# Turning the normalised rows of x by one DMA per tile instead of on TensorE, from tile 6 on

## The chip, the cores and the metric

The kernel runs on one core of a Trainium2 chip. The metric is the device time of one execution in microseconds (us). Engines are named as the profile names them: PE is TensorE's matmul side and PEld its weight load, DVE is VectorE, ACT is ScalarE, POOL is GpSimd, SP is SyncE, which here only issues DMAs.

## The reference

2048 tokens of width 512 pass through two gated blocks. The first picks one of four experts by token id, the second is a feed-forward block with fp8 weights.

```python
# xattn: ctx is Wg, Wu and Wd of each of 4 experts, (4, 512, 512)
n = layernorm(x)
for e in range(4):
    g = silu(n @ ctx[e].T); u = n @ ctx[e].T
    y = (g * u) @ ctx[e].T
    out = where(expert_of(token) == e, y, out)
x = x + tanh(g_xattn) * out
# ffn: weights rounded to fp8, per-column scales
n2 = layernorm(x)
x = x + tanh(g_ffn) * ((silu(n2 @ Wgate * gs) * (n2 @ Wup * us)) @ Wdown * ds)
```

## The kernel before, in words

All work is written out by hand, one in-order program for each engine, tied by counting semaphores. The tokens are first sorted by expert, so that each of 16 tiles of 128 tokens (`xs[:, tile]`, fp32, gathered by POOL) holds one expert or a border between two. The first block is then 19 **steps** (16 tiles and 3 borders). Both precisions are made by splitting: a value is a high fp16 part and a low fp16 part (the value less its high part), and a product is three fp16 products.

In step s PE does, in this order: `product_z(s)` (12 matmuls of 128x512, L1333); then, while s < 15, the four 128x128 fp32 transposes of the normalised tile s+1 from `xn` into the PSUM bank `XT` (`transpose4`, L1262, named `bank<-ident,xn`); the four transposes of `h` of step s-1 into `HT` (same line, `bank<-ident,h`); column norms of a weight slab (L1391); and `product_y(s-2)` (12 matmuls, L1314). `product_y(s-2)` waits for `x1_done`, which DVE raises with `add_expert(s-3)` (L1028) at the end of its own step s-1, because both use the one PSUM bank `Y`.

ACT's step s: `silu` (L738) when z(s) is there, `x_high(s+1)` (L681, the high part out of `XT` into `X2[:, s+1, 0]`), `normalise(s+2)` (L676, `xn`), `h_high(s-1)` (L744), then work on the fp8 slabs (L700, L708) and from step 7 the second layernorm (L691, L692). DVE's step s: `product_h` (L1099), `x1_low(s+1)` (L999, reads `XT` in PSUM and `X2`), `h_low(s-1)` (L995), `round_stats` (L978 and the small rows after it: one `bn_stats` of a tile ahead, for s+4 < 16, and from step 6 one for the second layernorm, so steps 6 to 11 have both), `slab_big` (L975) for each of that step's slabs (two in steps 5, 8, 11, 14, 16), and `add_expert(s-2)` (L1028).

POOL works off rounding of the slabs in the same steps: `round_slab` (L581 makes `w_sum` and raises `sum_done`, L584), `ln_scalars(s+4)` (L510, L513, waits for DVE's statistics), and from step 8 `x2_low` (L597).

SP issues every plain DMA and every DMA transpose in one order. After four slab loads come the 12 transposes of the experts' matrices (L438), each expert followed by a wait until they have landed; then for each step `turn_x2(s-8)` (L446, from step 8) and the loads of the step's slabs (`load_slab`, L428), of which load n waits for `sum_done` of slab n-4, whose buffer it fills. The first of these loads, slabs 4 and 5, belong to steps 2 and 3.

The second block (L1415 and L1423) follows: four groups of four tiles, one chain of matmuls. The first operand of `product_y(18)` and of these groups depends on DVE's `ffn_scales` and on `add_expert(17)`, which stand behind the end of POOL's slab work.

Of the kernel before, what the change touches and what calls it, by code (L numbers as in the profile page):

```python
# [16 lines left out]
F32, F16, BF16, I32 = mybir.dt.float32, mybir.dt.float16, mybir.dt.bfloat16, mybir.dt.int32  # L17
ALU = mybir.AluOpType
ACT = mybir.ActivationFunctionType
# [14 lines left out]
def build(nc, x, token_ids, ctx, g_xattn, g_ffn, gate_w, up_w, down_w, gate_scale, up_scale, down_scale, out):  # L34
    B, S, D = x.shape
    TOK = B * S
    TILES = TOK // P
# [9 lines left out]
    EARLY_NORMS = 18  # L47
    LATE_ORDER = ("g2", "d3", "g3", "d4", "g4", "g5", "d5", "g6", "g7", "d6", "d7", "d8", "d9", "d10", "d11")
    TURNS = {25: 11, 27: 12, 29: 13, 31: 14, 33: 15}
    STATS1_LEAD = 4  # L50
    STATS2_LAG = 6
    NORM2_LAG = 7
# [14 lines left out]
    with ExitStack() as stack:  # L67
# [3 lines left out]
        def sem(name):  # L71
            return stack.enter_context(nc.semaphore(name))


        xs = sb("xs", [P, TILES, D], F32)
        M = sb("M", [P, E, 2, KC, 512], F16)
        X2 = sb("X2", [P, TILES, 2, KC, P], F16)
# [182 lines left out]
        y_done = sem("y_done")  # L260
        x1_done = sem("x1_done")
        x2n_done = sem("x2n_done")
        x2T_in = [sem("x2T_in0"), sem("x2T_in1")]
        x2lo_done = sem("x2lo_done")
        abs_done = sem("abs_done")
# [48 lines left out]

        def x2_row(tile, part):
            return x2rows[:, tile % 2, part * D:(part + 1) * D]

        def x2_landed(engine, tile):

# [86 lines left out]
        def _(sp):  # L406
# [24 lines left out]
            def turn_expert(e):  # L431
# [8 lines left out]
                sp.wait_ge(m_in, 16 * KC * e)  # L440
                sp.nop().then_inc(m_ready, 1)

            def turn_x2(tile):

                sp.wait_ge(x2lo_done, tile + 1)
                sp.dma_start_transpose(X2[:, tile].rearrange("p a k i -> p (a k) i"),  # L446
                                       x2rows[:, tile % 2, :]).then_inc(x2T_in[tile % 2], 16)
# [4 lines left out]
            for e in range(1, E):  # L452
                turn_expert(e)
            for s in range(STEPS):
                if s >= X2_LAG:
                    turn_x2(s - X2_LAG)
                for n in slabs_of(s, s):
                    load_slab(loaded)
                    loaded += 1
# [185 lines left out]
        def _(act):  # L645
            a = nc.scalar
# [25 lines left out]
            def normalise(tile):  # L672
                act.wait_ge(ln_done, tile + 1)
                if tile:
                    act.wait_ge(xT_done, tile)
                a.activation(xn[:], xs[:, tile, :], ACT.Identity, scale=ln_tab[:, tile, 0, 0:1],  # L676
                             bias=ln_tab[:, tile, 0, 1:2]).then_inc(xn_done, 1)

            def x_high(tile):
                act.wait_ge(xT_done, tile + 1)  # L680
                a.activation(x2_part(tile, 0), XT[:].rearrange("p (k i) -> p k i", k=KC),  # L681
                             ACT.Copy).then_inc(xhi_done, 1)
# [57 lines left out]
            def h_high(s, lo):  # L740
                act.wait_ge(hT_done, s + 1)
                if lo >= 2:
                    act.wait_ge(y_done, s - 1)
                a.activation(hTh[:, lo % 2, :], HT[:], ACT.Copy).then_inc(hhi_done, 1)  # L744

            def step(s, lo):
                if lo < 2:
                    x_high(s + 1)
                silu(s, lo)
                if 2 <= lo < TILES - 1:  # L750
                    x_high(s + 1)
                if lo + 2 < TILES:
                    normalise(s + 2)
                if lo >= 1:
                    h_high(s - 1, lo - 1)
                if lo + 1 < E:
                    expert_rows_high(lo + 1)
                if lo == 0:
                    squares(3)
                for n in slabs_of(s, lo):  # L760
                    slab_abs(n, slab_slot(n), slab_turn(n), slab_before(n))
                for n in squared_of(s, lo):
                    slab_square(n, n % 2, n)
                if lo >= NORM2_LAG:
                    normalise2(s - NORM2_LAG)
# [74 lines left out]
        def _(dve):  # L840
# [152 lines left out]
            def h_low(s, lo):  # L993
                dve.wait_ge(hhi_done, s + 1)
                v.tensor_tensor(hTl[:, lo % 2, :], HT[:], hTh[:, lo % 2, :], ALU.subtract).then_inc(hlo_done, 1)  # L995

            def x1_low(tile):
                dve.wait_ge(xhi_done, tile + 1)
                v.tensor_tensor(x2_part(tile, 1), XT[:].rearrange("p (k i) -> p k i", k=KC), x2_part(tile, 0),  # L999
                                ALU.subtract).then_inc(xlo_done, 1)  # L1000
# [110 lines left out]
            def step(s, lo):  # L1111
# [2 lines left out]
                product_h(s, lo)  # L1114
                if lo == STEPS - 1:
                    ffn_norms(SMALL, 0, 2)
                if 2 <= lo < TILES - 1:
                    x1_low(s + 1)
                if lo >= 1:
                    h_low(s - 1, lo - 1)  # L1120
                if lo == STEPS - 1:
                    add_expert(s - 2)
                if lo == 0:
# [132 lines left out]
        def _(pe):  # L1256
# [69 lines left out]
                        for k in range(KC) for lhs, rhs in ((0, 0), (0, 1), (1, 0))]  # L1326

            def product_z(s, lo, operands):
                pe.wait_ge(xlo_done, min(s + 1, TILES))
                if lo >= 2:  # L1330
                    pe.wait_ge(h_done, s - 1)
                for n, (lhs, rhs) in enumerate(operands):
                    ins = t_.matmul(Z[lo % 2][:], lhs, rhs, start=(n == 0), stop=(n == 3 * KC - 1))  # L1333
                ins.then_inc(z_done, 1)
# [15 lines left out]
            def step(s, lo):  # L1350

                product_z(s, lo, z_next[0])
                if lo < TILES - 1:
                    pe.wait_ge(xn_done, s + 2)
                    transpose4(XT, xn, xT_done)
                if lo == 0:
# [151 lines left out]
```

## Time and profile before

| | us |
|---|---|
| median of 3 runs | 406.75 (406.28 to 407.37) |
| the profiled execution | 406.11 |
| its span | 404.4 |
| PE busy | 379.4 (94%) |
| DVE busy | 219.1 (54%) |
| ACT busy | 187.3 (46%) |
| POOL busy | 161.2 (40%) |

The profiled execution is 0.64 us under the median; 1.7 us of it lie outside the span. The shares are means over two unlike halves: until about 140 us the 19 steps run on all engines, after that PE works almost alone. The granted clock was 0.995 of full speed over the span.

### The profile page before, as it was taken

How to read it: one execution, taken by the hardware profiler on the slowest of the kernel's cores; microseconds unless marked ns; L12 is line 12 of the kernel's file. 1: busy time of each engine (PE TensorE's matmuls, PEld its weight loads, DVE VectorE, ACT ScalarE, POOL GpSimd, SP SyncE). 2: the span in 40 equal slices, each digit the busy share in tenths (PEclk: the TensorE clock that was granted, in tenths of full speed). 3: DMA queues.
4: the chain of work that ended last, by engine and by line, in shares of the span. 5: the costliest groups of instructions: out<-in, count | busy, mean ns of one | idle time of the engine just before them, and what ended most of it. 6: DMA issues, size and time to landing. Idle time of an engine off the chain costs nothing.

```text
span 404.4 us, 6038 instructions
## 1 busy us (share of the span) xinstructions
PE 379.4 (94%) x1912; PEld 183.2 (45%) x1912; DVE 219.1 (54%) x465; ACT 187.3 (46%) x294; POOL 161.2 (40%) x199
## 2 busy tenths in 40 slices
PE   2889799999999899999999999999999999999990
PEld 2445355545555444444444444444444444444440
DVE  5876888797867786787524222224222225222243
ACT  4777756787886536694432222222222222222220
POOL 2678989997989930411008100006200005300003
PEclk9999999999999999999999999999999999999997
DMA  7697783444445340670002000001100001100002
GB/s 259 167 343 196 138 193 113 68 117 80 105 105 117 94 104 2 151 165 25 0 2 78 28 0 0 2 0 53 52 0 0 0 0 40 66 0 2 0 0 104
DMA packets 40075, 29.99 MB, mean 74 GB/s; under 512 B 31192, under 2 KB 31216, under 8 KB 40048
## 3 DMA queue, kind: packets, MB, share of 16 engines
q1 hardware_dynamic: 37488, 21.26, 22.2%
q0 software_dynamic: 2560, 8.39, 6.1%
q8 instruction: 14, 0.23, 0.3%
q14 instruction: 13, 0.11, 0.1%
HBM read 18.11 MB, written 4.19 MB: 55 GB/s over the span
## 4 chain that ended last, share of the span: by engine, by line
PE 81%; DVE 8%; POOL 3%; issue 3%; ACT 2%; DMA 1%; DVEq 0%; POOLq 0%; ACTq 0%
PE bank L1415 41%; PE bank L1423 20%; PE bank L1314 9%; PE bank L1333 8%; PE bank L1262 2%; POOL xs L502 1%; DVE stats L978 1%; DMA xs<-in_x,order 1%; DVE row_hot L913 1%; ACT xn L676 1%; DVE xs L1243 1%; DVE hTl L995 1%; DVE X L1240 1%; DVE xs L1028 1%; ACT hTh L744 1%
## 5 line engine op out<-in xcount | busy, mean ns | idle before, releaser
L1415 PE MATMUL bank<-X,W 128*128 128x512 f16 (+1 forms) x768 | 173.3, 379 | 0.0
L1415 PEld LDWEIGHTS bank<-X,W 128*128 128x128 bf16 x768 | 75.0, 98 | 90.9 <-ACT late_norms L802 0.5
L1189 DVE SCALAR_TENSOR_TENSOR cs<-bank,up_mul,cs 128x512 f32<-128x512 f32 x48 | 36.0, 751 | 108.7 <-PE bank L1415 104.6
L1423 PE MATMUL bank<-W,cs 128*128 128x512 bf16 x376 | 88.7, 379 | 0.0
L776 ACT ACTIVATE cs<-bank,gate_mul 128x512 f32<-128x512 f32 x48 | 32.9, 686 | 80.0 <-PE bank L1415 80.0
L783 ACT ACTIVATE cs<-cs 128x512 f16<-128x512 f32 x47 | 29.5, 628 | 77.8 <-DVE cs L1189 77.6
L633 POOL TENSOR_TENSOR xs<-xs,X 128x512 f32<-128x512 f32 x12 | 15.3, 1274 | 125.2 <-DVE X L1240 124.9
L1423 PEld LDWEIGHTS bank<-W,cs 128*128 128x128 f16 x376 | 36.5, 98 | 43.7 <-DVE cs L1197 0.2
L1333 PE MATMUL bank<-M,X 128*128 (+1 forms) x228 | 52.3, 379 | 3.1 <-DVE X L999 2.1
L1197 DVE TENSOR_TENSOR cs<-cs 128x512 f16<-128x512 f32 x47 | 33.8, 719 | 31.5 <-ACT cs L783 31.5
L1314 PE MATMUL bank<-M,hTh 128*128 (+1 forms) x152 | 45.1, 378 | 3.2 <-DVE xs L1028 3.2
L639 POOL DMA_INDIRECT out<-xs,order x16 | 16.7, 1045 | 50.9 <-DVE xs L1243 47.5
L1333 PEld LDWEIGHTS bank<-M,X 128*128 (+1 forms) x228 | 22.2, 98 | 30.7 <-issue 5.3
L1314 PE MATMUL bank<-M,hTl 128*128 (+1 forms) x76 | 28.8, 379 | 0.0
L584 POOL TENSOR_TENSOR W<-w_sum,w_big 128x512 bf16<-128x512 f32 x21 | 27.0, 1286 | 1.6
L581 POOL TENSOR_TENSOR w_sum<-ws,w_big 128x512 f32<-128x512 f32 x21 | 26.7, 1271 | 0.7 <-POOL W L584 0.2
L510 POOL TENSOR_TENSOR ln_tab<-prep,ln_half 128x1 f32<-128x1 f32 (+1 forms) x26 | 16.6, 639 | 23.2 <-DVE prep L883 23.0
L738 ACT ACTIVATE silu_z<-bank,z_step 128x512 f32<-128x512 f32 x18 | 12.3, 685 | 23.9 <-PE bank L1333 23.9
L597 POOL TENSOR_TENSOR x2rows<-x2n,x2rows 128x512 f16<-128x512 f32 x16 | 19.3, 1208 | 7.2 <-ACT x2n L692 7.2
L700 ACT ACTIVATE w_big<-ws 128x512 f32<-128x512 f32 x36 | 21.4, 627 | 0.6 <-DMA ws<-in_L_ffn_up_w 0.6
L1314 PEld LDWEIGHTS bank<-M,hTh 128*128 128x128 f16 x152 | 13.6, 97 | 17.7 <-issue 3.9
L1099 DVE SCALAR_TENSOR_TENSOR h<-bank,h_step,silu_z 128x512 f32<-128x512 f32 x18 | 13.5, 750 | 14.8 <-PE bank L1262 8.7
(164 smaller groups left out, 379.8 us busy)
## 6 DMA issues: line engine op xcount, KB each, us to landing
ws<-in_L_ffn_gate_w SPq DMA_DIRECT2D x12, 256.0 KB, 2.7
ws<-in_L_ffn_up_w SPq DMA_DIRECT2D x12, 256.0 KB, 2.7
ws<-in_L_ffn_down_w SPq DMA_DIRECT2D x12, 256.0 KB, 2.9
cs<-in_ctx SPq DMA_DIRECT2D x2, 1024.0 KB, 6.6
X<-in_ctx SPq DMA_DIRECT2D x2, 1024.0 KB, 6.9
xs<-in_x,order POOLq DMA_INDIRECT x16, 4.3
dsc<-in_L_ffn_down_scale SPq DMA_DIRECT2D x1, 256.0 KB, 7.0
X<-x2rows SPq DMA_TRANSPOSE x16, 3.1
```

Source lines behind the costliest of these rows:

```text
L581: g.tensor_tensor(w_sum[:], ws[:, slot], w_big[:, slot], ALU.add).then_inc(sum_done, 1)
L584: g.tensor_tensor(dst, w_sum[:], w_big[:, slot], ALU.subtract).then_inc(q_done, 1)
L597: g.tensor_tensor(x2_row(tile, 1), x2n[:, tile % 2, :], x2_row(tile, 0), ALU.subtract).then_inc(x2lo_done, 1)
L700: a.activation(w_big[:, slot], ws[:, slot], ACT.Abs, scale=FP8_STEP).then_inc(abs_done, 1)
L776: a.activation(sg[:, c % 2, :], GATE[c % 2][:], ACT.Silu, scale=gate_mul[:, c:c + 1]).then_inc(sg_done, 1)
L783: a.activation(fuse_part(g, c, 0), fuse[:, c % 2, :], ACT.Copy).then_inc(fh_done, 1)
L1189: v.scalar_tensor_tensor(out=fuse[:, c % 2, :], in0=UP[c % 2][:], scalar=up_mul[:, c:c + 1], in1=sg[:, c % 2, :], op0=ALU.mult, op1=ALU.mu ...
L1197: v.tensor_tensor(fuse_part(g, c, 1), fuse[:, c % 2, :], fuse_part(g, c, 0), ALU.subtract).then_inc(fl_done, 1)
L1314: ins = t_.matmul(dst[:], lhs, expert_block(e, part, k), start=(n == 0), stop=(n == 3 * KC - 1))
L1333: ins = t_.matmul(Z[lo % 2][:], lhs, rhs, start=(n == 0), stop=(n == 3 * KC - 1))
L1415: ins = t_.matmul(dst[c % 2][:].rearrange("p (t i) -> p t i", t=TPG), w, x2_group(g, part, k), start=(k == 0 and part == 0), stop=(k == KC ...
L1423: ins = t_.matmul(ACC[t][:], fuse_part(g, c, part)[:, t * P:(t + 1) * P], W8[:, down_slab(c), :], start=(c == 0 and part == 0), stop=(c == ...
```

## The change

For tiles 6 to 15 PE no longer transposes. ACT writes the normalised row tile twice in token order (`split_rows`: once as fp16 into `x_row(tile, 0)`, once as fp32 into `xn`), DVE takes the fp16 part off (`x_row_low`, into `x_row(tile, 1)`), and one DMA transpose issued by SP (`turn_x`) writes both parts of the tile into `X2`. The buffers are the front of `cs`, whose first use is over by then. `x_high` and `x1_low` of those tiles fall away. `product_z` of those tiles waits for the DMA (`x_landed`) in place of `xlo_done`.

```diff
+    X_BY_DMA = 6
...
+        def x_row(tile, part):
+            return cs[:, 0, tile % 2].bitcast(F16)[:, part * D:(part + 1) * D]
...
+            def turn_x(tile):
+                sp.wait_ge(xrow_low_done, tile - X_BY_DMA + 1)
+                sp.dma_start_transpose(X2[:, tile].rearrange("p a k i -> p (a k) i"),
+                                       cs[:, 0, tile % 2].bitcast(F16)).then_inc(xT_in[tile % 2], 16)
...
             for s in range(STEPS):
+                if X_BY_DMA <= s + 2 < TILES:
+                    turn_x(s + 2)
                 if s >= X2_LAG:
                     turn_x2(s - X2_LAG)
...
+            def split_rows(tile):
+                act.wait_ge(ln_done, tile + 1)
+                if tile >= X_BY_DMA + 2:
+                    act.wait_ge(xT_in[tile % 2], 16 * ((tile - X_BY_DMA) // 2))
+                mul, add = ln_tab[:, tile, 0, 0:1], ln_tab[:, tile, 0, 1:2]
+                a.activation(x_row(tile, 0), xs[:, tile, :], ACT.Identity, scale=mul, bias=add)
+                if tile == X_BY_DMA:
+                    act.wait_ge(xT_done, tile)
+                else:
+                    act.wait_ge(xrow_low_done, tile - X_BY_DMA)
+                a.activation(xn[:], xs[:, tile, :], ACT.Identity, scale=mul, bias=add).then_inc(xn_done, 1)
...
-                if 2 <= lo < TILES - 1:
+                if 2 <= lo < X_BY_DMA - 1:
                     x_high(s + 1)
-                if lo + 2 < TILES:
+                if lo + 2 < X_BY_DMA:
                     normalise(s + 2)
                 if lo >= 1:
                     h_high(s - 1, lo - 1)
+                if X_BY_DMA <= lo + 2 < TILES:
+                    split_rows(s + 2)
...
+            def x_row_low(tile):
+                dve.wait_ge(xn_done, tile + 1)
+                v.tensor_tensor(x_row(tile, 1), xn[:], x_row(tile, 0), ALU.subtract).then_inc(xrow_low_done, 1)
...
-                if 2 <= lo < TILES - 1:
+                if 2 <= lo < X_BY_DMA - 1:
                     x1_low(s + 1)
                 if lo >= 1:
                     h_low(s - 1, lo - 1)
+                if X_BY_DMA <= lo + 2 < TILES:
+                    x_row_low(s + 2)
...
-                pe.wait_ge(xlo_done, min(s + 1, TILES))
+                pe.wait_ge(xlo_done, min(s + 1, X_BY_DMA))
+                if X_BY_DMA <= lo < TILES:
+                    x_landed(pe, s)
...
-                if lo < TILES - 1:
+                if lo < X_BY_DMA - 1:
                     pe.wait_ge(xn_done, s + 2)
                     transpose4(XT, xn, xT_done)
```

Three places show where instructions now stand. First SP, from the slab loads ahead of the experts' transposes (`M<-W`) on. Before:

```order
10 L428 DMA ws<-in_L_ffn_gate_w 128x512 x4
11 L438 DMA_TRANSPOSE M<-W 128x8x128 x12
12 L428 DMA ws<-in_L_ffn_up_w 128x512 x4
13 L428 DMA ws<-in_L_ffn_gate_w 128x512 x3
14 L446 DMA_TRANSPOSE X<-x2rows 128x8x128
15 L428 DMA ws<-in_L_ffn_gate_w 128x512
16 L428 DMA ws<-in_L_ffn_up_w 128x512
```

And with the change, the same stretch of SP (`X<-cs` is `turn_x`, tile 6 first):

```order
11 L450 DMA_TRANSPOSE M<-W 128x8x128 x12
12 L440 DMA ws<-in_L_ffn_up_w 128x512 x2
13 L458 DMA_TRANSPOSE X<-cs 128x8x128
14 L440 DMA ws<-in_L_ffn_up_w 128x512
15 L458 DMA_TRANSPOSE X<-cs 128x8x128
16 L440 DMA ws<-in_L_ffn_up_w 128x512
17 L440 DMA ws<-in_L_ffn_gate_w 128x512
18 L458 DMA_TRANSPOSE X<-cs 128x8x128
19 L440 DMA ws<-in_L_ffn_gate_w 128x512
```

Each tile's transpose stands between the slab loads: that of tile 6 behind the loads of slabs 4 and 5, that of tile 7 also behind that of slab 6, that of tile 8 also behind those of slabs 7 and 8.

Second DVE, one of its steps 6 to 11 (`hTl` is `h_low`, `X<-bank,X` is `x1_low`, `cs<-xn,cs` is `x_row_low`). Before:

```order
146 L1099 SCALAR_TENSOR_TENSOR h<-bank,h_step,silu_z 128x512
147 L999 TENSOR_TENSOR X<-bank,X 128x512
148 L995 TENSOR_TENSOR hTl<-bank,hTh 128x512
149 L978 BN_STATS stats<-xs 128x6 x2
150 L987 BN_AGGR mv<-stats 128x2 x2
```

With the change:

```order
147 L1138 SCALAR_TENSOR_TENSOR h<-bank,h_step,silu_z 128x512
148 L1030 TENSOR_TENSOR hTl<-bank,hTh 128x512
149 L1034 TENSOR_TENSOR cs<-xn,cs 128x512
150 L1013 BN_STATS stats<-xs 128x6 x2
151 L1022 BN_AGGR mv<-stats 128x2 x2
```

The count is the same. The subtraction that read PSUM is gone, and one that reads two SBUF tensors stands behind `h_low`, ahead of the statistics and of `add_expert`.

Third ACT, the front of the same step. Before:

```order
46 L738 ACTIVATE silu_z<-bank,z_step 128x512
47 L681 ACTIVATE X<-bank 128x512
48 L676 ACTIVATE xn<-xs,ln_tab 128x512
49 L744 ACTIVATE hTh<-bank 128x512
50 L700 ACTIVATE w_big<-ws 128x512
```

With the change:

```order
47 L771 ACTIVATE silu_z<-bank,z_step 128x512
48 L777 ACTIVATE hTh<-bank 128x512
49 L705 ACTIVATE cs<-xs,ln_tab 128x512
50 L710 ACTIVATE xn<-xs,ln_tab 128x512
51 L733 ACTIVATE w_big<-ws 128x512
```

`h_high` moves up to the second place; `xn` is finished by the fourth instruction of the step instead of the third.

## Rows read from the trace of the kernel before

**Rows 1.** The page's chain that ended last, shares by engine.

```profile
PE 81%; DVE 8%; POOL 3%; issue 3%; ACT 2%; DMA 1%; DVEq 0%; POOLq 0%; ACTq 0%
```

**Rows 2.** Timeline of PE, steps 6 to 8: start, length, line, names, count, idle before.

```profile
58.32 2.75 PE L1333 MATMUL bank<-M,X 128*128 x12
60.91 0.60 PE L1262 MATMUL bank<-ident,xn 128*128 128x128 f32 x4
61.35 0.60 PE L1262 MATMUL bank<-ident,h 128*128 128x128 f32 x4
...
67.07 0.60 PE L1262 MATMUL bank<-ident,xn 128*128 128x128 f32 x4
...
68.34 0.59 PE L1314 MATMUL bank<-M,hTh 128*128 x2 [0.15 <-DVE xs L1028]
...
70.92 2.75 PE L1333 MATMUL bank<-M,X 128*128 x12
```

**Rows 3.** Timeline of PE, the transposes of steps 13 and 15.

```profile
105.00 0.60 PE L1262 MATMUL bank<-ident,xn 128*128 128x128 f32 x4
...
117.40 0.60 PE L1262 MATMUL bank<-ident,h 128*128 128x128 f32 x4
```

**Rows 4.** Timeline of SP's DMA issues, 39 to 60 us.

```profile
54.94 2.03 SPq L428 DMA_DIRECT2D ws<-in_L_ffn_up_w  x2
```

**Rows 5.** Timeline of POOL, the sums of slabs 1 and 2.

```profile
55.34 1.27 POOL L581 TENSOR_TENSOR w_sum<-ws,w_big 128x512 f32<-128x512 f32 x1
...
61.26 1.27 POOL L581 TENSOR_TENSOR w_sum<-ws,w_big 128x512 f32<-128x512 f32 x1
```

**Rows 6.** The DMA transposes of `x2rows` (L446, 16 of them), issue to landing.

```profile
DMA to landing us min/median/max: 3.0/3.1/4.7
```

**Rows 7.** Timeline of DVE, step 7 (one slab, both statistics).

```profile
68.24 0.75 DVE L1099 SCALAR_TENSOR_TENSOR h<-bank,h_step,silu_z 128x512 f32<-128x512 f32 x1
...
69.66 0.69 DVE L995 TENSOR_TENSOR hTl<-bank,hTh 128x512 f16<-128x512 f32 x1
70.27 1.28 DVE L978 BATCH_NORM_STATS2 stats<-xs 128x6 f32<-128x512 f32 x2
...
72.19 0.41 DVE L975 TENSOR_SCALAR w_big<-w_big 128x512 f32<-128x512 f32 x1
72.73 0.75 DVE L1028 SCALAR_TENSOR_TENSOR xs<-bank,y_step,xs 128x512 f32 x1
```

**Rows 8.** Timeline of DVE, start of step 15, which has no transposes of x.

```profile
118.33 0.75 DVE L1099 SCALAR_TENSOR_TENSOR h<-bank,h_step,silu_z 128x512 f32<-128x512 f32 x1 [1.49 <-ACT silu_z L738]
```

**Rows 9.** Timeline of ACT, front of step 8.

```profile
73.71 0.69 ACT L738 ACTIVATE silu_z<-bank,z_step 128x512 f32<-128x512 f32 x1 [1.12 <-PE bank L1333]
74.30 0.59 ACT L681 ACTIVATE X<-bank 128x512 f16<-128x512 f32 x1
74.78 0.81 ACT L676 ACTIVATE xn<-xs,ln_tab 128x512 f32<-128x512 f32 x1
75.48 0.59 ACT L744 ACTIVATE hTh<-bank 128x512 f16<-128x512 f32 x1
```

**Rows 10.** Groups by line over the span: busy us, mean ns, idle before.

```profile
L1197 DVE TENSOR_TENSOR cs<-cs 128x512 f16<-128x512 f32 x47 | 33.8, 719 | 31.5 <-ACT cs L783 31.5
...
L975 DVE TENSOR_SCALAR w_big<-w_big 128x512 f32<-128x512 f32 x21 | 14.9, 728 | 0.5 <-ACT w_big L700 0.5
```

**Rows 11.** Timeline of DVE at 165 us.

```profile
165.05 1.64 DVE L1197 TENSOR_TENSOR cs<-cs 128x512 f16<-128x512 f32 x1
```

**Rows 12.** Timeline of POOL at 163 us.

```profile
163.42 2.72 POOL L597 TENSOR_TENSOR x2rows<-x2n,x2rows 128x512 f16<-128x512 f32 x2
169.33 1.16 POOL L597 TENSOR_TENSOR x2rows<-x2n,x2rows 128x512 f16<-128x512 f32 x1 [3.19 <-ACT x2n L692]
```

**Rows 13.** Timeline of DVE, `add_expert(17)`.

```profile
144.61 0.74 DVE L1028 SCALAR_TENSOR_TENSOR xs<-bank,y_step,xs 128x512 f32 x1
```

**Rows 14.** Timeline of PE, start of `product_y(18)`.

```profile
146.30 0.59 PE L1314 MATMUL bank<-M,hTh 128*128 x2
```

More of the change, by code:

```diff
@@ L262, in build @@
         x2n_done = sem("x2n_done")
+        xT_in = [sem("xT_in0"), sem("xT_in1")]
+        xrow_done = sem("xrow_done")
+        xrow_low_done = sem("xrow_low_done")
         x2T_in = [sem("x2T_in0"), sem("x2T_in1")]
@@ L316, in x2_row, with x_landed @@
             return x2rows[:, tile % 2, part * D:(part + 1) * D]
+        def x_row(tile, part):
+            return cs[:, 0, tile % 2].bitcast(F16)[:, part * D:(part + 1) * D]
+        def x_landed(engine, tile):
+            for slot in range(2):
+                engine.wait_ge(xT_in[slot], 16 * ((tile - slot) // 2 - (X_BY_DMA - slot + 1) // 2 + 1))
         def x2_landed(engine, tile):
```

## The prediction, made before the changed kernel ran

> **What bounds the kernel now.** I read the chain that ended last first. It is 81% PE [rows 1], so in most places only time taken from PE, or given to it as a wait, moves the end. Then the timeline of PE in the steps that change. T(s) is here the moment when `product_z(s)` has been issued and the transposes start. T(6) is 60.91 and T(7) 67.07, a step of 6.16 us without a gap; z takes 2.59 (58.32 to 60.91) and y 2.58 (68.34 to 70.92) [rows 2]. So y starts 6.16 - 2.59 - 2.58 = 0.99 after T. In step 7 it did not start at 67.07 + 0.99 = 68.06 but at 68.34, behind DVE's `add_expert` [rows 2]. That is the point to watch: PE is the bound, and DVE is close behind it. The timeline of DVE gives the size: in step 7 the add ends at 72.73 + 0.75 = 73.48 [rows 7], T(7) + 6.41, and 0.15 later PE can start (the idle time that the row of 68.34 names [rows 2]). PE would want to start at T + 6.16 + 0.99 = T + 7.15. The slack is 0.6 us where `slab_big` has its short 0.41 [rows 7], and less where it takes its mean of 0.728 [rows 10].
>
> **What is removed.** Ten groups of four transposes. One costs 61.35 - 60.91 = 0.44 us of PE [rows 2], together 4.4. If PE stayed the bound, a step would be 5.72, and the kernel 4.4 us shorter. `x_high` and `x1_low` also go, ten times each; ACT gets one row write more than it loses.
>
> **First cost: tile 6 arrives late.** Before, `XT` was ready half a step ahead. Now z(6) waits for a DMA that SP issues, and SP works in order. Its loads of slabs 4 and 5 end at 54.94 + 2.03 = 56.97 [rows 4]; the second waits for POOL's sum of slab 1, which ends at 55.34 + 1.27 = 56.61 [rows 5]. Only then comes `turn_x(6)`. A transpose of the same shape lands 3.1 us after its issue [rows 6], here at 60.1. z(6) started at 58.32 [rows 2], and without tile 6's transposes PE would want it at 57.9. PE waits 2.2, and T(6) is 60.1 + 2.59 = 62.7, 1.8 later than before. Bounds: the landing has 3.0 to 4.7 [rows 6], so 1.7 to 3.4 later. Nothing hides it: what follows on PE needs the same z. The row work itself is in time (`x_row_low(6)` comes in DVE's step 4, some microseconds ahead of 57).
>
> `turn_x(7)` stands behind the load of slab 6, that waits for the sum of slab 2, 61.26 + 1.27 = 62.5 [rows 5]. With 0.36 for the load's issue (56.97 - 56.61) it is issued at 62.9, lands at 66.0, and T(7) = 68.6. PE alone would have 62.7 + 5.72 = 68.4. So T(7) is 1.5 later than before.
>
> **Second cost: DVE's add comes later against a shorter PE step.** I follow one step from T.
> - ACT: silu starts 0.20 after T(8) = 70.92 + 2.59 = 73.51, the next instruction 0.59 after it [rows 9]. That is now `h_high`, T + 0.79. The fp16 row follows 0.48 later (74.78 - 74.30), the fp32 row `xn` 0.70 after that (75.48 - 74.78) and takes 0.81 [rows 9]: done at T + 2.78.
> - DVE: `product_h` starts at T + 0.93, as in step 15 (118.33 - 117.40) [rows 3, 8], where there are no transposes of x either; `h_low` is through some 1.3 later, at T + 2.2 (twice about 0.65). Then it stands still for `xn` until T + 2.85. The subtraction takes 0.61, as `h_low` does (70.27 - 69.66 [rows 7]), plus a cost c, below. From the statistics to the end of the add it is 73.48 - 70.27 = 3.21 [rows 7], with `slab_big` at its shortest; its mean is 0.32 over that [rows 10], and steps 6 to 11 hold 8 slabs: c2 = 0.42 a step. So the add ends at T + 6.67 + c + c2.
> - PE now wants y at T + 5.72 + 0.55 = T + 6.27, and gets it at T + 6.82 + c + c2. Even with no contention it waits 0.55. From there y and z bring T(s+2) = T(s) + 11.99 + c + c2, a step of 6.0 + (c + c2)/2.
>
> **The unknown cost c.** The trace of before has no subtraction of two SBUF tensors on DVE while POOL is busy in these steps. The nearest row is the same operation and shape in the second block: 0.719 on the mean [rows 10], but 1.64 at 165.05 [rows 11], where POOL ran two `x2_low`, 163.42 to 166.14 [rows 12]. It ended 0.55 after POOL's second. So c is 0 when it meets a gap and 0.95 at worst. POOL instructions of 1.27 [rows 5] follow one another closely here, and a start at a random point of one waits for half of it: I take c = 0.5. `h_low`, which reads PSUM as `x1_low` does, takes 0.69 [rows 7] in the midst of POOL's work, so what is removed paid no such cost.
>
> The Trainium skill ("SBUF — State Buffer", section "Who interferes with whom") speaks against this change: a VectorE instruction with two SBUF inputs and a GpSimd instruction that reads SBUF exclude each other, whoever comes second is blocked until the other ends. The row of 1.64 agrees. By that rule alone the wait could be a whole POOL instruction, and the sum would be about 2 us higher than mine.
>
> **The sum.** A step in the stretch T(7) to T(13) is (11.99 + 0.5 + 0.42)/2 = 6.46. T(13) = 68.6 + 6 x 6.46 = 107.4; before it was 105.00 [rows 3]: 2.4 later. Steps 12 and 13 have one statistic less, 0.64 (half of 1.28 [rows 7]): two steps are 11.35 + 0.92 = 12.27 against 117.40 - 105.00 = 12.40 [rows 3]. T(15) is 2.2 later. From step 15 nothing is changed, and the second block follows at its own pace. In its front, `add_expert(17)` ends at 144.61 + 0.74 = 145.35 [rows 13] and `product_y(18)` starts at 146.30 [rows 14]: 0.95 of slack behind POOL's work. POOL loses time to the new subtraction as well (two `x2_low` took 2.72 instead of 2 x 1.16 [rows 12]: 0.40), ten times at most, 4.0. PE is 2.2 later itself, which with 0.95 covers 3.2: between 0 and 0.9 comes on top, and I take 0, since not every one collides. Sum: -4.4 of transposes, +6.6 of waits, **+2.2 us**.
>
> The profiled execution had 406.11, so the next would have 408.3. It lay 0.64 under the median of 406.75, so I forecast a median of **409.0 us**. What this kernel's measurement can tell from no change is about 0.3%, 1.2 us.
>
> Bounds of the terms: c from 0 to 0.95 moves T(15) by -2.0 to +1.8; c2 at 0 takes 1.7 off, at 0.8 adds 1.5; the landing -0.1 to +1.6, of which DVE's slack absorbs none.
>
> **The rivals.**
> - *No change, about 407.* The subtraction meets POOL's gaps (c = 0). A step is 6.2, T(13) = 105.8, T(15) = 117.6, 0.2 later than before: tile 6's wait eats exactly what is left of the gain. For it: `slab_big`, which meets POOL too, goes through at its shortest in step 7 [rows 7]. Against: the 1.64.
> - *Faster, about 404.* The add keeps up, because `xn` and the subtraction come earlier than I count them (`h_low` is 0.6 earlier than before, and when DVE is late it no longer waits for `xn`). Then PE runs at 5.72: T(15) = 68.6 + 8 x 5.72 = 114.4 against 117.40, 3.0 less. It decides from an add that ends at T + 6.12 or earlier, 0.55 before my shortest. If SP also had tile 6 there in time, the full 4.4 would come, 402.4. Against it is the arithmetic of ACT: two rows of 0.7 have to be written ahead of one subtraction.
> - *Much slower, about 412.* The transposes of x stand behind loads that wait for POOL's sums. If POOL loses 0.4 at each collision and the DMAs land in 4.7, z waits for tiles 8, 11 and 14 too: 1.6 more at tile 6 and some 2 more behind it. For it: POOL is the busiest engine beside PE here. Against: from tile 9 on I count more than 1 us between landing and use.
>
> **How the numbers follow.** My forecast 50%, no change 20%, faster 18%, much slower 12%. The forecast's own range is 407.9 to 411.2. The range for 8 in 10 takes in no change and the nearer part of the two outer cases: 404.5 to 411.8. Faster by over 0.3%: 0.18; within: 0.20; slower: 0.62.
>
> **What would show it.** PE waits some 2 us ahead of z(6), released by the DMA `X<-cs`. PE's wait ahead of y, released by `add_expert`, comes in most of the steps 7 to 13, where now it is 0.15 in step 7. The new subtraction has a mean of about 1.2 us, not 0.69, and PE's transposes are 40 fewer. I am wrong if z(6) finds its tile, if the subtraction stays at 0.69, or if steps 6 to 12 are clearly under 6.2.

## The result, and the profile after

The changed kernel takes 414.57 us (median of 6 runs, 412.57 to 418.47) beside 406.69 (6 runs, 406.11 to 408.16): a ratio of 1.020 [1.017, 1.022], 7.9 us slower where I had forecast 2.3. Its profiled execution had 417.02 us with a span of 415.3, beside 406.11 and 404.4. Two executions ran in a slower state and are left out of the medians: 417.25 us of run 4 below (run 11's expectation, with its 413.46 for run 4, still has it in) and 413.70 us of the kernel before beside runs 5 to 8.

The page of the changed kernel: the lines of busy time and the chain that ended last.

```profile
PE 379.5 (91%) x1851; PEld 180.3 (43%) x1872; DVE 223.7 (54%) x465; ACT 189.9 (46%) x294; POOL 164.9 (40%) x199
...
PE 76%; DVE 10%; issue 5%; ACT 3%; POOL 3%; DMA 1%; DVEq 0%; ACTq 0%; POOLq 0%
```

PE's share of the chain fell from 81% [rows 1] to 76%. PE is as busy in all as before, with forty transposes fewer: some of its instructions must have got slower. The view of what PE waits for says where it stands still (us in total, times, longest):

```profile
PE bank L1355 <- DVE xs L1067: 7.3, 8, 2.5
PE bank L1376 <- issue: 5.4, 4, 3.9
...
PE bank L1303 <- DVE hTl L1030: 2.2, 1, 2.2
```

L1355 is `product_y`, L1376 `product_z`, L1303 the transposes; L1067 is `add_expert`. The timelines of PE and SP give the places.

```profile
63.83 4.45 PE L1376 MATMUL bank<-M,X 128*128 x12 [3.89 <-issue]
68.11 0.60 PE L1303 MATMUL bank<-ident,h 128*128 128x128 f32 x4
...
95.20 0.59 PE L1355 MATMUL bank<-M,hTh 128*128 x2 [1.65 <-DVE xs L1067]
...
148.80 0.63 PE L1303 MATMUL bank<-ident,h 128*128 128x128 f32 x4 [2.17 <-DVE hTl L1030]
```

```profile
56.33 2.88 SPq L440 DMA_DIRECT2D ws<-in_L_ffn_up_w  x2
59.26 1.23 SPq L458 DMA_TRANSPOSE X<-cs  x1
```

The view of the line L458, which issues all ten of these DMAs, sums up their landing:

```profile
DMA to landing us min/median/max: 3.0/3.4/3.9
```

z(6) starts 3.89 us late. That is 4.6 after its DMA's issue at 59.26, which stands behind the loads of slabs 4 and 5. Taken for each DMA alone, the view has a landing for five of the ten only, and tile 6's is not among them. In runs 3, 5, 14 and 15 below tile 6's is known (6.8, 3.8, 5.3 and 3.5 us), and z(6) starts 0.6 after it each time; by that estimate it was 4.0 here. Then z itself takes 68.11 - 63.83 = 4.28 us where it took 2.59 [rows 2]. The view of windows tells why (each row ends with the granted clock, the share of the DMA engines and GB/s): PE is busy all through each of these stretches at hardly more than half speed.

```profile
20.00:24.00 4.00, 4.00 (x15) 1.75 (x13) 2.00 (x13) 0.29 (x1) 2.88 (x5) 0.58 0.95 337
64.00:68.00 4.00, 4.00 (x12) 1.54 (x12) 0.00 (x0) 0.00 (x0) 3.84 (x6) 0.57 0.61 155
149.00:153.00 4.00, 3.97 (x13) 1.49 (x12) 3.69 (x11) 1.63 (x3) 3.83 (x6) 0.59 0.15 30
```

The account of the span's 10.9 us, along T:

| where | us |
|---|---|
| lower clock at 20 to 24, ahead of anything changed | 1.6 |
| z(6) waits | 3.9 |
| z(6) runs at the lower clock, 4.28 - 2.59 | 1.7 |
| T(6) to T(15): 126.1 - 68.1 = 58.0, before 117.4 - 60.9 = 56.5 (nine times 0.44 less of transposes, and more waits for adds) | 1.5 |
| the wait for `hTl` at the walk's end, 2.17 where it was 1.66 | 0.5 |
| lower clock at 149 to 153, y(17) 4.27 where it was 2.59 | 1.7 |

The 0.44 of tile 6's own transposes is not seen in it: it is used up by small waits ahead of z(6).

The 0.5 at the walk's end comes from one small DVE instruction, which takes twice as long. It ends both times when POOL's sum of a slab does (137.1 and 146.3). Run 8, whose subtraction doesn't meet POOL's reads, has the same 1.01. In DVE's timeline of the kernel before and of the changed one:

```profile
136.63 0.49 DVE L1046 TENSOR_TENSOR nn<-col_ssq 128x8 f32<-128x8 f32 x1
```

```profile
145.31 1.01 DVE L1085 TENSOR_TENSOR nn<-col_ssq 128x8 f32<-128x8 f32 x1
```

The first line of the table isn't the change's. Executions of the kernel before have mean clocks from 0.995 down to 0.987, and all but two of their times lie within 2.2 us; the changed kernel's six had 0.980 to 0.989. The two profiled executions give a price: three stretches at the lower clock for 0.995 - 0.980, so 0.005 each, at 1.7 us. By that estimate the changed kernel's six have 2.1 stretches on the mean (0.9845), the 70 executions of the kernel before that stand beside the experiments 0.8 (0.991), and some 2.2 of the 7.9 us between the medians are that. It is a rough one: the kernel before at 0.987 is only 1.2 us slower than at 0.995, where this price would give 2.7.

### The profile page after: what moved, and what is told of

Its sections match the earlier page's. It is cut to its first block, busy times and chain, and to the rows that moved or that the text cites. A ratio compares the mean times of both kernels' runs of the same rounds, so it can differ in the third digit from the quotient of the medians.

```text
span 415.3 us, 5955 instructions
## 1 busy us (share of the span) xinstructions
PE 379.5 (91%) x1851; PEld 180.3 (43%) x1872; DVE 223.7 (54%) x465; ACT 189.9 (46%) x294; POOL 164.9 (40%) x199
## 4 chain that ended last, share of the span: by engine, by line
PE 76%; DVE 10%; issue 5%; ACT 3%; POOL 3%; DMA 1%; DVEq 0%; ACTq 0%; POOLq 0%
PE bank L1458 40%; PE bank L1466 19%; PE bank L1355 8%; PE bank L1376 8%; DVE stats L1013 1%; DVE cs L1034 1%; POOL xs L522 1%; DVE xs L1067 1%; PE bank L1303 1%; DMA xs<-in_x,order 1%; ACT cs L705 1%; DVE row_hot L948 1%; ACT xn L710 1%; DVE xs L1284 1%; DVE X L1281 1%
## 5 line engine op out<-in xcount | busy, mean ns | idle before, releaser
L1466 PE MATMUL bank<-W,cs 128*128 128x512 bf16 x355 | 86.2, 379 | 1.1
L1376 PE MATMUL bank<-M,X 128*128 (+1 forms) x228 | 55.7, 397 | 7.8 <-issue 5.4
L1355 PE MATMUL bank<-M,hTh 128*128 (+1 forms) x152 | 46.3, 387 | 7.4 <-DVE xs L1067 7.3
L1376 PEld LDWEIGHTS bank<-M,X 128*128 (+1 forms) x228 | 23.0, 101 | 38.0 <-issue 15.0
L1355 PE MATMUL bank<-M,hTl 128*128 (+1 forms) x76 | 29.5, 389 | 0.0
L604 POOL TENSOR_TENSOR W<-w_sum,w_big 128x512 bf16<-128x512 f32 x21 | 28.4, 1353 | 1.6
L1355 PEld LDWEIGHTS bank<-M,hTh 128*128 128x128 f16 x152 | 13.9, 99 | 23.2 <-issue 10.1
```

Of the source, the lines that this page charges most:

```text
L604: g.tensor_tensor(dst, w_sum[:], w_big[:, slot], ALU.subtract).then_inc(q_done, 1)
L1355: ins = t_.matmul(dst[:], lhs, expert_block(e, part, k), start=(n == 0), stop=(n == 3 * KC - 1))
L1466: ins = t_.matmul(ACC[t][:], fuse_part(g, c, part)[:, t * P:(t + 1) * P], W8[:, down_slab(c), :], start=(c == 0 and part == 0), stop=(c == ...
```

## The experiments

My theory, A: two separate costs. Tile 6's row lands late, and the wait brings a stretch at the lower granted clock; and `x_row_low` is slow beside POOL's reads (1.17 us), so that every `add_expert` behind it is late. The rivals, B: the row's way through ACT, DVE and a DMA is too long in itself, or one of the two costs is all.

The edits, from which the kernels are put together:

```diff
# first 9
-    X_BY_DMA = 6
+    X_BY_DMA = 9
# PSUM: the fp32 row goes to the bank XT, free by then
-                a.activation(xn[:], xs[:, tile, :], ...)
+                a.activation(XT[:], xs[:, tile, :], ...)
# (and the first such row waits until DVE has read XT)
-                    act.wait_ge(xT_done, tile)
+                    act.wait_ge(xlo_done, tile)
-                v.tensor_tensor(x_row(tile, 1), xn[:], x_row(tile, 0), ...)
+                v.tensor_tensor(x_row(tile, 1), XT[:], x_row(tile, 0), ...)
# SP6: tile 6's DMA ahead of slab loads 4 and 5
+            turn_x(X_BY_DMA)
             for s in range(STEPS):
-                if X_BY_DMA <= s + 2 < TILES:
+                if X_BY_DMA < s + 2 < TILES:
                     turn_x(s + 2)
# SP order: each tile's DMA ahead of the loads of the step before
-                if X_BY_DMA <= s + 2 < TILES:
-                    turn_x(s + 2)
                 if s >= X2_LAG:
                     turn_x2(s - X2_LAG)
+                if X_BY_DMA <= s + 3 < TILES:
+                    turn_x(s + 3)
# early add in steps a to b: ahead of round_stats and slab_big,
# and the call behind them falls away in these steps
-                if lo == STEPS - 1:
+                if a <= lo <= b or lo == STEPS - 1:
                     add_expert(s - 2)
```

| kernel | us, median (range) | ratio to before, 95% |
|---|---|---|
| 1. first 9 | 410.88 (410.87 to 413.75) | 1.011 [1.007, 1.016] |
| 2. 16 more matmuls ahead of z(6) | 414.10 (413.32 to 415.59) | 1.018 [1.015, 1.021] |
| 3. PSUM | 415.21 (413.71 to 416.74) | 1.018 [1.015, 1.021] |
| 4. SP6 | 412.81 (410.85 to 414.11) | 1.011 [1.007, 1.015] |
| 5. early add, steps 4 to 18 | 412.94 (411.94 to 413.87) | 1.014 [1.010, 1.018] |
| 6. first 9, PSUM, early add 4 to 18 | 408.70 (407.14 to 409.52) | 1.003 [1.001, 1.005] |
| 7. before, early add 4 to 18 | 409.32 (407.53 to 409.75) | 1.005 [1.003, 1.007] |
| 8. first 9, PSUM | 407.89 (406.10 to 409.56) | 1.002 [1.000, 1.004] |
| 9. first 9, PSUM, early add 4 to 15, SP order | 406.32 (404.70 to 406.65) | 0.998 [0.996, 1.001] |
| 10. before, early add 4 to 15 | 409.03 (407.53 to 410.10) | 1.005 [1.003, 1.008] |
| 11. PSUM, SP6 | 408.69 (408.54 to 408.87) | 1.005 [1.003, 1.007] |
| 12. first 9, PSUM, early add 4 to 15 | 407.83 (407.17 to 408.66) | 1.003 [1.001, 1.005] |
| 13. first 9, PSUM, SP order | 407.75 (405.94 to 408.07) | 1.001 [0.999, 1.003] |
| 14. PSUM, SP order | 411.76 (409.81 to 415.10) | 1.011 [1.007, 1.014] |
| 15. SP order | 415.50 (412.37 to 417.01) | 1.018 [1.013, 1.022] |
| 16. first 9, PSUM, early add 9 to 15, SP order | 404.92 (404.53 to 406.45) | 0.996 [0.995, 0.998] |

The kernel before had medians of 406.5 to 407.3 beside them.

### Tile 6: runs 1, 2, 4 and 15

Run 1. 

> The changed kernel with tiles 9 to 15 turned by DMA instead of 6 to 15 (the transposes of 6, 7 and 8 are back on TensorE). Theory A, late first tile: the loss is z(6) waiting 3.9 us for its DMA, plus 1.7 us of lower granted clock behind that wait, plus about 1 us of longer steps behind. Tile 9's DMA is issued with time to spare, so no wait ahead of z(9) and no clock fall there: 7 x 0.44 = 3.1 us of transposes less, about 3.5 us of waits for the add more, 407 us (406 to 408.5). Theory B, each tile costs by itself (SBUF port and DMA load): 7 of the 10 tiles keep 7/10 of the 7.9 us, 412 us.

A tile that lands in a quieter stretch isn't waited for: z(9) has no wait, and the time falls by 3.7 us though three tiles fewer profit. Theory B's number was nearer, since the adds' waits stay. Their largest is the same as in the changed kernel, in PE's timeline of run 1:

```profile
90.72 0.59 PE L1355 MATMUL bank<-M,hTh 128*128 x2 [1.65 <-DVE xs L1067]
```

Run 2, with `for i in range(16): t_.matmul(bank[7][:], row_hot[:, 0, :], ...)` ahead of the wait of z(6); bank 7 isn't read. 

> The changed kernel with 16 matmuls without use put on TensorE ahead of product_z(6), so that TensorE works (16 x 0.216 = 3.5 us) instead of standing idle until tile 6 lands. Theory A: z(6) starts at the same time but takes 2.6 us instead of 4.3, granted clock 1.0 there, and the whole is 1.3 to 1.7 us shorter, about 413 us. Theory B: the lower clock has no part in it, no change, 414.6 us.

In PE's timeline the added matmuls fill the wait, and z(6) has its 2.59 us back. The window shows the granted clock (1.00) at the same place.

```profile
59.41 3.62 PE L1373 MATMUL bank<-row_hot 128*128 128x512 f16 x16
62.86 2.75 PE L1380 MATMUL bank<-M,X 128*128 x12
65.45 0.60 PE L1303 MATMUL bank<-ident,h 128*128 128x128 f32 x4
...
59.00:66.00 7.00, 7.00 (x40) 3.50 (x39) 3.00 (x8) 1.69 (x4) 6.43 (x9) 1.00 0.79 203
```

So in this trace the slow z(6) came from the idle stretch ahead of it, not from its operands or the DMAs beside it. The median moves by only 0.5, within its range. A part of the 1.7 is lost again by the filling itself: with the early stretch of 1.6 taken off, z(6) of the changed kernel starts at 62.2 and here at 62.86, so that T(6) is 65.45 instead of 66.5. The profiled execution also had a stretch at the lower clock at 44 to 48 us. Where the rest went stays open.

Run 4. 

> The changed kernel with the DMA transpose of tile 6 issued on SP ahead of the loads of slabs 4 and 5 instead of behind them. Theory A: it is issued about 2.9 us earlier, z(6) waits 1 us or less instead of 3.9, and no clock falls behind it: 4 to 5 us less, 410 us. Theory B: the wait is exchanged for waits elsewhere (SP's loads come later, POOL and DVE are as loaded), less than 1.5 us gained, 413 us or more.

The time is between the two numbers, just under B's, with executions 3 us apart. But at tile 6 the trace has what A said: issued at 56.88, z(6) waits 0.94 and is not slowed. (Some 1.2 us of the shorter wait are PE's own lateness, from a stretch at the lower clock at 44 to 48.) What B said is there too: SP's next three loads hold it for 5.56 us, tile 7's DMA behind them is issued at 63.76, and z(7) and z(8) wait 1.56 and 0.78. SP's timeline and PE's:

```profile
56.88 1.23 SPq L458 DMA_TRANSPOSE X<-cs  x1
...
60.52 0.82 PE L1377 MATMUL bank<-M,X 128*128 x3 [0.94 <-issue]
```

Run 15. 

> The changed kernel with SP's order alone altered, for every tile from 6 on; the float32 row stays in SBUF, where its subtraction meets POOL's reads. The changed kernel took 414.6 us. Theory A (two separate costs, tile 6's wait with the lower granted clock behind it, and the adds made late by the subtraction of 1.17 us): this gives back the first only, 411; the adds keep 3 to 4.6 us. Theory B (SP's order is all of it): 408.5 or less. Theory C (it costs the slab chain as much): 414.

Theory C, 415.5: nothing gained. `turn_x(6)` now stands behind slab load 4 only, but it isn't issued earlier: at 57.76, where the changed kernel has 59.26 less the early stretch of 1.6. Slab load 4 itself goes at 57.37 only, because SP waits 3.9 us for the experts' transposes to land. PE's timeline says z(6) still starts 4.1 us after the issue, waits 3.48, and is slow:

```profile
61.82 4.41 PE L1376 MATMUL bank<-M,X 128*128 x12 [3.48 <-issue]
```

From issue to z's start it is 3.6 us in run 4, 4.1 here, 4.4 in run 11, 4.6 in the changed kernel, 5.9 in run 14 and 7.4 in run 3. The way of a row that is issued behind the experts' transposes and among the slab loads has no constant length, and by its rows of windows the changed kernel's DMA engines are full there (the same columns as above, 0.90):

```profile
52.00:60.00 8.00, 7.81 (x42) 3.68 (x39) 6.68 (x15) 5.44 (x9) 7.28 (x8) 1.00 0.90 193
```

Nor has the moment at which the experts' transposes have landed. In the profiled executions of the kernels that have no early stretch at the lower clock before it, SP gets to its next DMA between 54.94 (the kernel before) and 57.74 (run 8). Runs 8 and 13 do the same up to there, and have 57.74 and 55.17. I took 54.94 for given, and it is a value of one execution.

### The subtraction beside POOL: runs 3, 8, 11, 13 and 14

Run 3. 

> The changed kernel with the fp32 row written by ScalarE into the free PSUM bank XT instead of SBUF xn, so that the new subtraction on VectorE reads one SBUF and one PSUM tensor. Theory A: the subtraction falls from 1.17 to 0.69 us on the mean, adds come 0.5 us earlier, a step in the stretch 6 to 13 is 0.24 shorter: about 2 us less, 412.6 us, and z(6) still waits over 3 us. Theory B: the port is what costs, at most 409 us.

The groups by line of the changed kernel, then of run 3: with an operand in PSUM the subtraction takes what `h_low` takes.

```profile
L1034 DVE TENSOR_TENSOR cs<-xn,cs 128x512 f16<-128x512 f32 x10 | 11.7, 1166 | 3.6 <-ACT xn L710 3.6
```

```profile
L1034 DVE TENSOR_TENSOR cs<-bank,cs 128x512 f16<-128x512 f32 x10 | 6.9, 689 | 3.8 <-ACT bank L710 3.8
```

T(6) to T(15) falls from 58.0 to 55.1 us, by 2.9 where A wanted about 2. The total doesn't: here z(6) waited 8.43 us in the profiled execution, since SP waited 5.0 us for the experts' transposes (slab load 4 was issued at 60.10, not 56.33), and tile 6's own landing took 6.8. PE's timeline:

```profile
68.38 4.18 PE L1376 MATMUL bank<-M,X 128*128 x12 [8.43 <-issue]
```

Run 8. 

> Tiles 9 to 15 by DMA and the fp32 row in the PSUM bank XT, add_expert where it was. Theory A: against 410.9 us with the row in SBUF the subtraction loses its 0.48 us of port wait, so each add is that much earlier; 1.5 to 2.5 us less, 409 us. Theory C: no change.

Without the crowded tiles the same edit is worth its size: 410.88 to 407.89, 3.0 us.

Run 11. 

> The changed kernel with two of its three costs mended together: the float32 row in PSUM (subtraction 0.69 us where it took 1.17) and tile 6's transposing DMA ahead of the slab loads 4 and 5. Theory A (the three costs are separate and add up: adds about 2.9 us, tile 6's wait of z and the lower granted clock behind it): the one with SP's order alone took 413.46, so 410.6. Theory B (what one wait gives back the next takes, since a finished row or z still waits for a landing DMA, as in the run with tile 9, PSUM and the early add): 412 or more.

408.69, under even theory A's number, with four runs within 0.4 us and a clock of 0.992 to 0.993. The two edits that alone gave -1.8 and +0.6 give -5.9 together. Not all of that is shown to be theirs: in this trace the experts' transposes had landed by 54.99, when tile 6's DMA went, and by 56.88 only in run 4's. z(6) and z(7) still wait, and no fall of the clock follows this time; z(7) is behind three slab loads that hold SP for 6.83 us. PE's timeline and SP's:

```profile
59.38 2.76 PE L1377 MATMUL bank<-M,X 128*128 x12 [1.11 <-issue]
...
67.25 2.76 PE L1377 MATMUL bank<-M,X 128*128 x12 [1.99 <-DMA X<-cs]
```

```profile
54.99 1.24 SPq L458 DMA_TRANSPOSE X<-cs  x1
56.27 6.83 SPq L440 DMA_DIRECT2D ws<-in_L_ffn_up_w  x3
63.15 1.23 SPq L458 DMA_TRANSPOSE X<-cs  x1
```

Run 14. 

> The changed kernel from tile 6 on, with the float32 row in PSUM and with every tile's transposing DMA ahead of the slab loads of the step before (with tile 6's alone moved it took 408.69 us, with z waiting 1.11, 1.99 and 0.47 us at tiles 6, 7 and 8, the second behind a slab load that held SP for 6.8 us). Theory A (SP's order is the cost that is left): z(7)'s 1.99 and z(8)'s 0.47 go, 406.3 us. Theory B (the landing under the experts' transposes and slab loads is): 408.5, as before this edit.

Neither: 3.1 us worse than run 11. Tile 6's DMA is again behind slab load 4 (58.09 instead of 54.99), and the wait with its slow z are back. But SP's order is only 0.4 of these 3.1 us. The rest is there already when SP gets to slab load 4, by its timeline and by the view of what it waits for:

```profile
57.71 0.34 SPq L440 DMA_DIRECT2D ws<-in_L_ffn_up_w  x1
58.09 1.23 SPq L458 DMA_TRANSPOSE X<-cs  x1
```

```profile
SPq L453 <- DMA M<-W: 4.5, 1, 4.5
```

L453 stands right behind the wait for the experts' transposes. After it, tile 6's DMA takes 5.3 us to land. PE's timeline, and the window:

```profile
64.00 5.30 PE L1376 MATMUL bank<-M,X 128*128 x12 [5.94 <-issue]
...
62.00:69.00 7.00, 5.00 (x12) 1.96 (x13) 1.41 (x2) 0.00 (x0) 6.54 (x8) 0.53 0.65 148
```

The rest of the walk is as in run 3, 55.1 us from T(6) to T(15). What one slab load ahead of tile 6's DMA costs isn't settled by this pair: all seven executions of run 14 have a lower mean clock (0.980 to 0.985) than the four of run 11, so a long wait at z(6) is likely in all of them, and whether the order brings it through a slower landing stays open. Run 13 asks about the order of the other tiles.

Run 13. 

> First tile by DMA is 9, the float32 row is in PSUM, SP issues a tile's transposing DMA ahead of the slab loads of the step before, and the add stands where it stood (behind the statistics). Theory A (what is left of the changed kernel's cost with this first tile is SP's order and the adds, and the early add is a loss of its own, 1.5 to 2 us in the kernel before): 7 x 0.44 = 3.1 us saved, less the adds' waits of the run with tile 9 and PSUM (0.64 + 0.40 + 1.36 + 0.37, where the kernel before has 0.15 + 0.38), 2.2, and less what SP's order gives at tiles 11 and 13: 406 us, at or a little under before (407). Theory B (the early add was needed, as the adds now come 1.4 us late at more tiles): 408 or more.

407.75 beside run 8's 407.89, no difference, and nearer to B's number. PE waits for adds (1.29, 1.08, 0.36), never for a row: with first tile 9 and the late adds, SP's order is hidden.

### The add: runs 5, 6, 7, 9, 10, 12 and 16

Run 5. 

> The changed kernel with add_expert (VectorE) moved ahead of the layernorm statistics of the same step, from step 4 on. Theory A (late adds): the waits ahead of product_y for the add, 4.6 us in steps 7 to 14 of the profile of the change, go. VectorE's own work in a step of two statistics is 5.24 + 0.48 of port wait + some for slab_big, about 6.1 us, more than TensorE's 5.72, so part comes back: 2 to 4 us less than 414.6, 411.5. The wait for tile 6 and the clock behind it stay. Theory C (the steps are longer because DMAs of tiles 7 to 15 land late): no change.

1.6 us better, 1.4 short of A. The adds' waits in the changed part are gone, and rows take their place: z(8) waits 1.16, z(11) 1.83 and z(14) 2.11 us, and z(14) then runs at the lower clock (4.45 in its row). z(6) waits 2.72 and is not slowed. SP's timeline ahead of z(14): the row's DMA goes right behind a slab load, which waited for POOL's sum.

```profile
109.75 0.33 SPq L440 DMA_DIRECT2D ws<-in_L_ffn_gate_w  x1
110.12 1.23 SPq L458 DMA_TRANSPOSE X<-cs  x1
```

Run 6. 

> Three edits together: tiles 9 to 15 by DMA instead of 6 to 15, the fp32 row in the PSUM bank XT, add_expert ahead of the statistics. Theory A: no late tile, no port wait of the subtraction, no late add; what is left is 7 x 0.44 = 3.1 us of transposes less than before, 403.7 us (402.5 to 405.5), faster than both kernels. Theory C, or a cost of the DMA path that is none of these: 406.5 us or more.

Theory A missed by 5. z(11) waits 0.85 and z(14) 1.36 us for their rows, and the early add costs something by itself:

Run 7. 

> The kernel before with add_expert ahead of the statistics from step 4 on, nothing else: the control for the two others. Its waits for the add after step 4 are 0.5 us in all, so 0 to 0.7 us less, 406.3 us, no measurable change. If it gains more, the gain of the others is not one that turns on the change.

2.2 us slower than before, not faster. At a like clock it is less: its four executions at 0.993 take 407.5 to 407.7, some 1.5 over the profiled execution of the kernel before at 0.995, and the six at 0.988 to 0.989 take 409.3 to 409.8. In the profiled one, of 407.53, y(18) waits 1.43 us at the walk's end, for an add now behind a slab's work. Run 10 leaves the end as it was:

> The kernel before with the add ahead of the statistics in steps 4 to 15 only. With it in all steps to 17 the time was 409.32 us, and y(18) waited 1.43 us for an add that came behind a slab's W, where the kernel before waits nowhere. If that is what it cost, this kernel is at the 407.0 us of before (within 0.5); if the early add costs something all along the walk, 408.5 or more.

It doesn't give them back. The add now stands ahead of `x1_low` of the tile that PE wants next: z(6) waits 0.83 and z(11) 0.63 for it. And at the walk's end the small rows of `late_norms` met POOL's work in the profiled execution. In DVE's timeline two instructions on 128x8 elements take 1.27 and 1.12 us, like ones 0.17 (before, the first of them took 1.23 and the second 0.17), and the wait for `hTl` is 3.12 us:

```profile
140.06 0.16 DVE L1047 TENSOR_TENSOR gu<-gs,us 128x8 f32<-128x8 f32 x1
140.25 1.27 DVE L1048 TENSOR_TENSOR gu<-gu 128x8 f32<-128x8 f32 x1
141.56 0.17 DVE L1049 TENSOR_TENSOR b<-nn,gu 128x8 f32<-128x8 f32 x1
141.76 1.12 DVE L1050 TENSOR_SCALAR b2c<-b 128x8 f32<-128x8 f32 x1
```

Run 12. 

> As the one with SP's changed order, but with SP's order left as it was: first tile 9, PSUM, early add in steps 4 to 15. Theory A: the waits ahead of z(11) and z(13) stay (2.2 to 2.5 us of the 3.1 us saved), and the 2 us that the early add cost at the end of the walk (the wait of y(18), 1.43 us, in the kernel before with the early add) are gone: 406.3 us. Theory B (the waits ahead of z were chance): 404.5.

Run 9. 

> First tile by DMA is 9, the float32 row is written to PSUM, the add of step s-1's experts stands ahead of the round's statistics in steps 4 to 15 only, and SP issues a tile's transposing DMA ahead of the slab loads of the step before, where it stood behind them. In the run with tile 9, PSUM and the early add, two waits of PE ahead of z are left (0.85 us at tile 11 and 1.36 us at tile 13), and there SP's own rows show the DMA of tile 13 issued at 106.77 right behind a slab load at 106.40 that waited for POOL's sum, while the row was finished at 103.84. Theory A (SP's queue: a finished row waits behind a slab load that waits for POOL): both waits go; 7 x 0.44 = 3.1 us of transposes come off whole, less some 0.5: about 404.5 us beside a kernel before of 407. Theory B (the DMA itself, or the row on DVE, is too late; SP's order is beside the point, or the loads that now stand behind it delay POOL's sums as much): 406.5 or more.

(The expectation of run 9 says tile 13 where the trace has tile 14.) Run 12 keeps waits of 1.52, 0.37 and 0.82 us ahead of z(11), z(13) and z(14), as A said, but is at 407.8, not 406.3: the early add's cost isn't that of the walk's end alone. Run 9 has none of them from tile 9 on and is 1.5 us faster: there the cause of these waits was SP's order. It stays 1.8 over A's number, with the 0.83 at z(6).

Run 16. 

> First tile 9, float32 row in PSUM, SP's order altered, and the add ahead of the statistics in steps 9 to 15 alone. With it ahead in steps 4 to 15 the time was 406.32 us; there z(6) waited 0.83 us for DVE's low half of tile 6, which the early add stands ahead of, and after step 9 no such instruction is left, since those rows go by DMA. Theory A (the early add costs only where DVE still has a low half of x to make for PE; from step 9 it only takes the adds' waits away): 0.83 us come back and the 1.29 and 1.08 us waits of the run without the early add go at least in part: 405.3 us, 1.6 us under before. Theory B (what limits is something else, the wait of 2.2 us for hTl at the end of the walk and the granted clock after it): 406.3 or more.

404.92 beside 406.52: theory A, and faster than the kernel before by 1.6 us. From T(9) to T(15) PE goes at 5.7 to 5.8 us a step. The view of what PE waits for:

```profile
PE bank L1355 <- DVE xs L1067: 4.9, 5, 2.5
...
PE bank L1376 <- DVE X L1038: 2.1, 2, 1.5
...
PE bank L1303 <- DVE hTl L1030: 0.4, 1, 0.4
```

Of the 3.1 us that seven tiles could save, half arrives.

## Why the prediction was wrong, point by point

The sign and the likeliest mechanism held; the size did not. At T(15) the trace is 7.1 us late (126.1 - 117.4 - 1.6 of the early stretch) where I had 2.2.

- **What is removed**: right. From T(15) on steps are as before, and where nothing waits in the changed part (T(9) to T(15) in run 16) a step is 5.72 to 5.8.
- **The first cost, "tile 6 arrives late"**: the step that failed. I had PE wait 2.2 us and T(6) 1.8 late; it waited 3.9, and T(6) is 5.6 late (68.1 - 60.9 - 1.6). The chain was right (slab loads, POOL's sum, then the DMA), its times too short. The issue at 59.26 is 57.7 without the early stretch, where I had 57.0, and z starts 4.6 after it instead of 3.1: 2.1 us together. I took the median landing from the transposes of `x2rows`, of which the first is issued at 78 us; tile 6's runs where the DMA engines are 0.90 busy. The landing was some 4.0 by the estimate above, and 0.6 more passed until z started, for which I had nothing. The bound of 4.7 from issue to landing [rows 6] would have covered both here, but not in runs 3 and 14, where the landing alone was 6.8 and 5.3. The other 1.7 is z at the lower clock, for which the sum had no term. Run 2 shows it gone when the idle stretch is filled; runs 4, 5 and 11 have shorter waits ahead of z(6) and no fall.
- **`turn_x(7)` behind slab 6**: it didn't decide. T(6) to T(7) is 5.72, PE's own time; T(6) was already that late.
- **The second cost, the adds**: right, a little small. T(7) to T(13) is 39.5 us, 6.58 a step where I had 6.46. Half of that is a slip of my sum: steps 8 and 11 have a second `slab_big`, and c2 holds only its 0.32 over the shortest, not the whole. (8 x 0.728 - 6 x 0.41)/6 is 0.56 instead of 0.42, a step of 6.53. T(13) to T(15) is 12.8 where I had 12.27. Run 3 gives 2.9 us back by taking the mean c out, and runs 1 and 8 3.0.
- **The unknown cost c**: right on the mean, 1.166 - 0.689 = 0.48 us beside 0.5. The rule of the Trainium skill ("SBUF — State Buffer", section "Who interferes with whom") bears the edit out in run 3: with one operand in PSUM the cost is gone. Its worst case, the wait for a whole POOL instruction (1.27 us), came in no row: the longest subtraction took 1.57 us, 0.88 over 0.69, and in run 1 one took 1.75.
- **The end of the walk at 0**: too small in the profiled execution. 0.5 of waiting for `hTl`, with 1.7 of the lower clock behind it. It wasn't POOL's lost time, as I had argued, but one DVE instruction of 128x8 that took 1.01 instead of 0.49, and run 8 has it with the subtraction's cost taken out.
- **The rivals.** "Much slower, about 412" was nearest, and for its first reason: the DMA landed late at tile 6. Of the tiles 8, 11 and 14 only the last one's z waited, 0.59, behind the late adds; with earlier adds (runs 5, 6 and 12) those of 11 and 14 did, and in run 5 that of 8. I gave it 12% because I took tile 6's wait as a sum of medians; an issue in a crowded stretch with nothing to cover it should have been taken at the bound at least.

What stays open is where in an execution the clock falls, how much of each median that makes up, and why the experts' transposes land up to 3 us apart in kernels that are alike up to there.

## What to carry to other kernels

When a DMA takes over from an engine, the first one, issued into the busiest stretch and behind other loads in its queue, needs its own sum, by the slowest landing that the trace has and not the median, and with the spread of what stands ahead of it in the queue; starting the change three tiles later was worth 3.7 us here. Give a DVE instruction that must run beside POOL one operand in PSUM (1.17 to 0.69 us). Mend all costs of such a change before judging it: single edits that kept tile 6 moved the time by -1.8 to +0.9 us, two together by -5.9, and with four the change became a gain of 0.4%.

## What the runs showed of the hardware that was not expected

- Behind a wait of PE the granted clock can fall to half (2.4 to 1.2 GHz) for 3 to 4 us (7 in runs 3 and 14), which cost about 1.7 us where a z or y fell into it, and 2.5 in run 14 (z(6) took 5.09). Ahead of z(6) waits of 3.48, 3.89, 5.94 and 8.43 us each had such a fall (in the last two the windows show the lower clock already inside the wait), waits of 0.94, 1.11 and 2.72 there, and of 1.56 and 1.99 ahead of z(7), had none. It isn't certain at a given length: at the walk's end waits of 2.15 to 2.19 us were followed by a fall in the changed kernel and runs 4, 8, 13, 14 and 15, but not in runs 1, 2, 3 and 11; one of 2.11 ahead of z(14) in run 5 was, and one of 3.12 in run 10 wasn't. Short waits aren't safe either. All 18 profiled executions have a wait of 1.5 us ahead of z(0) and one of 2.5 us ahead of the y at 43 to 45 us; a fall followed the first in four of them (the changed kernel and runs 1, 3 and 6) and the second in seven (runs 2, 4, 5, 9, 10, 12 and 16).
- On DVE an instruction of 0.17 us can take 1.0 to 1.3 beside POOL, whose instructions there take 1.26 to 1.27. Such collisions don't average out: the same wait of 1.65 us ahead of the same y came in the changed kernel and in runs 1, 2, 4 and 15. That DVE and POOL both run in step with PE would explain it, and no run tests it.
- A transposing DMA of one shape landed 3.0 to 3.1 us after its issue for all seven tiles of run 16, up to 3.9 for the five tiles of the changed kernel that the view has, and 5.3 and 6.8 for tile 6 in runs 14 and 3, where it was issued right behind the experts' transposes. Those landed late too: SP waited 1.9 us for them in the kernel before, 3.9, 4.5 and 5.0 in runs 15, 14 and 3.
